# Slot attention: the third tanh moves half a batch later, and VectorE forms the exponents of three of twelve chunks

## The reference

```python
Pn = rmsnorm(P, input_norm_w)              # P: 16 batches x 1500 keys x 128
k_proj = Pn @ Wk.T
v_proj = Pn @ Wv.T
for _ in range(3):
    sn = rmsnorm(slots, slot_norm_w)       # slots: 16 batches x 56 x 128
    q_proj = sn @ Wq.T
    scores = einsum('bkd,bmd->bkm', q_proj, k_proj) * SCALE
    attn = softmax(scores, axis=-2)        # over the 56 slots, for every key
    attn = attn / (sum(attn, axis=-1) + EPS)
    updates = einsum('bkm,bmd->bkd', attn, v_proj)
    slots = gru_cell(updates, slots, ...)  # two sigmoids (as tanh) and a tanh
```

## Time and profile before

| | |
|---|---|
| time, median of 3 runs | 579.34 us (575.66 to 580.33) |
| the profiled execution | 580.25 us, its span 578.4 us |
| slot attention in it | from about 240 us to about 464 us |
| TensorE busy over the span | 443.8 us (77%) |
| VectorE busy | 334.4 us (58%) |
| ScalarE busy | 315.0 us (54%) |
| GpSimd busy | 260.3 us (45%) |

### The profile page before, as it was taken

The page is one execution under the profiler, slowest core; times in us unless marked ns, Lnnn a source line. Parts: engine busy times, 40 slices in busy tenths (PEclk is TensorE's granted clock), DMA queues, the critical chain, the costliest instruction groups (busy, mean ns, idle before and its releaser), DMA issues.

```text
span 578.4 us, 17285 instructions
## 1 busy us (share of the span) xinstructions
PE 443.8 (77%) x6312; PEld 335.0 (58%) x6312; DVE 334.4 (58%) x916; ACT 315.0 (54%) x905; POOL 260.3 (45%) x476
## 2 busy tenths in 40 slices
PE   2893988889679999669999988899998574059910
PEld 1631324556554454458888878888898443049910
DVE  0669964677734655357777766777777326014512
ACT  1573673555412222099999988899999221025400
POOL 9294762223420000236776777766776500700044
PEclk9696996999896999689999999999999855569965
DMA  8862644444149911500000299300000397130112
GB/s 308 304 227 87 218 160 123 135 135 135 54 130 344 342 46 37 255 2 3 3 2 0 82 344 326 118 3 2 0 0 2 124 425 324 55 87 22 40 50 69
DMA packets 47346, 74.10 MB, mean 128 GB/s; under 512 B 4428, under 2 KB 40828, under 8 KB 46140
## 3 DMA queue, kind: packets, MB, share of 16 engines
q1 hardware_dynamic: 42796, 60.51, 31.5%
q0 software_dynamic: 1472, 8.72, 4.2%
q10 hardware_dynamic: 3024, 4.13, 2.3%
HBM read 69.75 MB, written 3.60 MB: 127 GB/s over the span
## 4 chain that ended last, share of the span: by engine, by line
PE 55%; DVE 18%; POOL 9%; issue 7%; ACT 5%; DMA 3%; ACTq 1%; POOLq 1%; DVEq 1%; SPq 0%
PE ps L1582 12%; PE ps L1566 8%; PE ps L1500 5%; PE ps L1408 4%; DVE ps L1207 4%; PE ps L1696 3%; PE ps L1708 3%; PE ps L1516 2%; DVE sm L1218 2%; POOL work L712 2%; POOL xe_scratch L753 2%; PE ps L1380 2%; POOL early_w L758 2%; PE ps L1480 2%; PE ps L1590 1%
## 5 line engine op out<-in xcount | busy, mean ns | idle before, releaser
L867 ACT ACTIVATE work<-ps,nb,rkey 125x56 f32<-125x56 f32 x576 | 173.5, 447 | 5.5 <-DVE nb L1211 5.5
L1566 PE MATMUL ps<-work,region 128*61 128x56 f32 (+1 forms) x2304 | 77.8, 224 | 6.9 <-ACT work L867 5.0
L1566 PEld LDWEIGHTS ps<-work,region 128*61 128x61 f32 (+1 forms) x2304 | 75.6, 140 | 7.5 <-issue 7.4
L1582 PE MATMUL ps<-region,work 125*64 125x129 f32 x1152 | 71.5, 279 | 6.4 <-POOL work L712 3.1
L1582 PEld LDWEIGHTS ps<-region,work 125*64 125x64 f32 x1152 | 65.1, 139 | 11.8 <-POOL work L712 9.3
L712 POOL TENSOR_TENSOR work<-work,rs 125x336 f32<-125x336 f32 x96 | 69.9, 749 | 3.8
L1207 DVE TENSOR_REDUCE ps<-ps 125x12 f32<-125x672 f32 x48 | 41.6, 866 | 36.9 <-PE ps L1566 36.8
L1218 DVE TENSOR_REDUCE sm<-work 125x12 f32<-125x672 f32 x48 | 40.6, 845 | 5.1 <-ACT work L867 4.6
L1408 PE MATMUL ps<-xln,folded 128*128 128x448 f32 x64 | 29.9, 592 | 10.2 <-ACT region L793 10.2
L758 POOL DMA_INDIRECT early_w<-ys_scratch,gidx x14 | 13.3, 950 | 52.1 <-DMA ys_scratch<-folded 48.1
L778 ACT ACTIVATE region<-early_w 125x1536 f32<-125x1536 f32 x16 | 23.7, 1490 | 17.1 <-DVE sumsq L987 12.9
(11 more groups left out here) (290 smaller groups left out, 972.6 us busy)
## 6 DMA issues: line engine op xcount, KB each, us to landing
early_w<-in_ctx SPq DMA_DIRECT2D x16, 768.0 KB, 4.8
region<-in_ctx SPq DMA_DIRECT2D x16, 768.0 KB, 9.4
region<-in_w SPq DMA_DIRECT2D x6, 2048.0 KB, 18.7
region<-in_ctxT SPq DMA_DIRECT2D x16, 750.0 KB, 11.0
work<-in_ctxT_blk SPq DMA_DIRECT2D x22, 187.5 KB
early_w<-in_w POOLq DMA_DIRECT2D x1, 4096.0 KB, 12.3
region<-in_ctx_blk ACTq DMA_DIRECT2D x11, 192.0 KB, 2.8
early_w<-in_ctx_blk ACTq DMA_DIRECT2D x10, 192.0 KB, 2.4
```

The lines of the kernel that those rows point to most:

```text
L867: i = act.activation(shares_of(u, a)[:, h, c, :], ps[:CP, 2 + 2 * a + h, c * S:(c + 1) * S], ACT.Exp, bias=nb[:, a, q:q + 1], scale=rkey[: ...
L1566: mm = pe.matmul(ps[r0:r1, 2 + 2 * a + h, c * S:(c + 1) * S], keysT[:, s, q * CP + r0:q * CP + r1], qT[:, p, a * S:(a + 1) * S], start=Tru ...
L1582: mm = pe.matmul(ps[i * COL:(i + 1) * COL, 6, 0:KW], A[:CP, u, i, h, c * S:c * S + COL], keys[:CP, 2 * p + i, h * CH + c, :], start=(h == ...
```

## The change

Three things are changed, all in slot attention.

1. For the last three chunks of the second half (`BYV = 3`), VectorE works out the exponent, score times `rkey` plus `nb`, right behind `nb` in `maxima`, with one instruction for each chunk, from PSUM into the place of the shares. ScalarE then takes one exponential over these 125 x 168 numbers in place, without scale or bias. A new semaphore `a_lin` tells ScalarE that they are there.
2. `candidate_of`, the third tanh, stands behind the first half of batch 1 on ScalarE, not ahead of it.
3. At the end of a round, `gru_inputs` stands ahead of `slot_mean` on VectorE, and `gru_start` ahead of `slot_proj` on TensorE.

```diff
+BYV = 3
...
+        a_lin = sem("a_lin")
...
                     act.wait_ge(a_neg, n + 1)
                     if later(w, 2):
                         act.wait_ge(u_mm, (w - 1) * 2)
-                for c in range(CH):
+                if h == 1:
+                    act.wait_ge(a_lin, n + 1)
+                for c in range(CH - BYV * h):
                     q = h * CH + c
                     i = act.activation(shares_of(u, a)[:, h, c, :], ps[:CP, 2 + 2 * a + h, c * S:(c + 1) * S], ACT.Exp,
                                        bias=nb[:, a, q:q + 1], scale=rkey[:, b, q:q + 1])
                 if h == 1:
-                    i.then_inc(a_exp, 1)
+                    act.activation(shares_of(u, a)[:, 1, CH - BYV:, :], shares_of(u, a)[:, 1, CH - BYV:, :], ACT.Exp).then_inc(a_exp, 1)
...
                 if now:
                     exponentials(now, v_, 0, 1)
+                    exponentials(now, v_, 1, 0)
                 if old:
                     candidate_of(v_ - 2)
                 if now:
-                    exponentials(now, v_, 1, 0)
                     exponentials(now, v_, 1, 1)
...
                 v.scalar_tensor_tensor(nb[:, a, :], mx, -1.0, rkey[:, b, :], ALU.mult, ALU.mult).then_inc(a_neg, 1)
+                v.wait_ge(a_neg, n + 1)
+                if later(w, 2):
+                    v.wait_ge(u_mm, (w - 1) * 2)
+                for c in range(CH - BYV, CH):
+                    lin = v.tensor_scalar(shares_of(u, a)[:, 1, c, :], ps[:CP, 3 + 2 * a, c * S:(c + 1) * S],
+                                          rkey[:, b, CH + c:CH + c + 1], nb[:, a, CH + c:CH + c + 1], ALU.mult, ALU.add)
+                lin.then_inc(a_lin, 1)
...
                 if following:
                     maxima(following, v_ + 1, 0)
+                if last:
+                    gru_inputs(v_ - 1)
                 if renews(g, c):
                     slot_mean(v_ + 2, c % 2)
-                if last:
-                    gru_inputs(v_ - 1)
...
                 if following:
                     scores(following, v_ + 1, 0)
+                if last:
+                    gru_start(v_ - 1, last[1])
                 if renews(g, c):
                     slot_proj(v_ + 2, (c + 2) % TWO, c % 2)
-                if last:
-                    gru_start(v_ - 1, last[1])
```

## The result

The changed kernel took **591.02 us** (median of 4 runs, 590.24 to 591.74), the kernel before, run beside it, 579.22 us (median of 4). The ratio of the times is **1.0234**, with a 95% interval from 1.0197 to 1.0271. The profiled execution has a span of 589.9 us against 578.4 before: 11.5 us more. The ratios in this text are those on record, with their intervals from single runs; they are not quotients of the medians beside them (here 591.02 / 579.22 = 1.0204) and differ from these by up to 0.4%.

A forecast was written before the change was run, and what follows sets the result against it. The bound was taken to be a chain of waits through TensorE, VectorE and GpSimd, 8.32 us a round, without ScalarE. 22 x 0.50 = 11.0, less 0.6 and 0.7, gave +9.7 us: 589.5 us, range 583.5 to 597.

The forecast's parts named there:

- The price of an instruction: Three new VectorE instructions between `nb` and the sum: 0.155 us each, with the wait 0.50 us a round (0.24 to 0.75).
- 22 rounds: Middle rounds of slot attention: each grows by 0.50 us, 22 x 0.50 = 11.0 us in all.
- second rival: Three instructions cheap, or swallowed in rounds around the change of groups: +3 to +5.8 us, 582 to 585; chance 0.12.
- The beginning: TensorE's 4.68 us wait for the first twelve exponentials: nine and a wide one take 2.99 us, saving 0.6 us.
- The end: Last round, where ScalarE ends last: the sum starts at about 449.7, not 450.43, saving 0.7 us, its own 0.50 included.
- Batch 1's three cost nothing: Middle of VectorE's round: 0.65 us idle ahead of L1207 covers 0.50; at the upper price 0.10 us a round lacks.
- GRU inputs ahead of `ss`, and TensorE's path with `F1w`: End of a round: no gain for the sum; `F1w` products start 0.43 us later, hidden as the chain moves 0.50.
- The third tanh: ScalarE, behind batch 1's `nb`: 0.8 us later, without cost, as new slots and squares have 0.79 us to spare.
- ScalarE: Wide exponential taken at 0.35 us; saves 1.1 us a round off the chain; about 2 us idle a round.
- ScalarE as the bound: ScalarE's 18.03 of 20 us busy sets the round, so relieving it makes the kernel faster, about 571 us; chance 0.05.
- A fallen clock: TensorE idles 0.5 us more a round and its clock falls: over 3 us each round struck, beyond 600; chance 0.04.
- The late slots: Later tanh meets busier GpSimd at group ends, `slot_proj` delays TensorE: 8 rounds by 0.5 to 1 us, 594 to 598; chance 0.06.

The follow-up runs named there:

- batch 0 alone: The changed kernel with exponents on VectorE for batch 0 only, twelve small exponentials on ScalarE for batch 1: 592.82 us, ratio 1.0265.
- batch 1 alone: The changed kernel with exponents on VectorE for batch 1 only, twelve small exponentials on ScalarE for batch 0: 577.11 us, ratio 0.9989.
- behind the sum: The changed kernel with batch 0's three VectorE instructions put after the sum of batch 1, the work the same: 576.35 us, ratio 0.9988.
- the moves alone: The changed kernel with all exponentials on ScalarE as before; third tanh, GRU inputs and GRU start stay moved: 577.55 us, ratio 0.9985.
- constants for both operands: The changed kernel with `rkey` and `nb` replaced by constants in the three VectorE instructions: 584.55 us, ratio 1.0165.
- the split inputs: All exponentials on ScalarE, orders as changed, but second GRU input after sum and `slot_norm`, third gate's product after scores and queries: 575.49 us, ratio 0.997.
- the exponents alone: The changed kernel with its three reorderings undone, keeping the exponents on VectorE and the wide exponential: 591.99 us, ratio 1.0256.

## Why the prediction was right, and where not

- **What bounds the kernel, and by what the change is slower: right.** The exponents lie between `nb` of batch 0 and the sum of batch 1, and that place alone pays (batch 0 alone 1.0265, batch 1 alone 0.9989, behind the sum 0.9988).
- **The price of an instruction: wrong.** The step that failed is "(0.24 + 0.07) / 2 = 0.155 us", a mean between 112 elements and one. The rows of 56 elements say 0.247 us, just above its upper end. It took the number of elements as all that differs, and the three instructions with constants or operands show that operands count as much: 0.123 us for none, and about 0.06 for each. In the kernel's text the GRU input that was taken as one end has one such operand (`wkey`), `ss`, the other end, has none, only a constant: their mean is the price of an instruction with half an operand. As an estimate, one and a half more at 0.06 add 0.09, and 0.155 + 0.09 = 0.245 us stands against 0.247 measured. So the round grew by 0.77 us and not by 0.50, and the sum stands 1.49 us behind `nb` and not some 1.2.
- **The rule that was weighed beside it**, of the Trainium skill (VectorE: DVE Perf Modes, section "The TRN2 errata"), gives 0.18 us as an estimate. The measurement agrees where one operand has a value for each partition (0.187 us), and differs for none (0.123) and for the two of this change (0.247).
- **22 rounds: the other error, which takes back half of the first.** The sum had 22 x 0.50 = 11.0 us; the rows say 14.16. By the true price it would have been 22 x 0.77 = 16.9, that is 5.9 more than forecast, and 2.8 us of that were not charged: 2.3 in the four rounds at the change of groups, 0.5 in the longer round of the loop. The prediction had this in its second rival ("some rounds around the change of groups, where TensorE stops for other reasons") but not in the sum. That the pauses there swallow the delay is read from the distances; no experiment isolates it.
- **The beginning: right**, -0.48 us against -0.6. TensorE's wait of 4.68 us there became two, 0.90 and 3.18, together 0.60 less. Another 0.70 was gone before the part began, where nothing is changed; that is a difference between two executions, not the change's.
- **The end: wrong.** The forecast was -0.7 because the sum would come sooner behind the exponentials. It did not. VectorE's and TensorE's steps of the GRU ended last instead: the wide exponential was done by 462.10, the sum started at 463.62 right behind the second GRU input, and from update 22 to update 23 it took 465.92 - 457.93 = 7.99 us, 7.82 before. The kernel before already had that input just ahead of the sum of 450.43 in the earlier trace rows (first row; the others are the changed kernel's):

```profile
450.04 0.32 DVE L1236 TENSOR_SCALAR work<-ps,bhh 128x112 f32<-128x112 f32 x1
```

```profile
463.37 0.33 DVE L1247 TENSOR_SCALAR work<-ps,bhh 128x112 f32<-128x112 f32 x1
463.62 0.84 DVE L1229 TENSOR_REDUCE sm<-work 125x12 f32<-125x672 f32 x1
```

  At 0.24 us for the input, the sum could have started at 450.28 at the earliest, whatever ScalarE saved: 0.15 us sooner and not 0.7. The 1.44 us that this stretch did gain came from the last update, which took 2.88 us and not 4.49, at another granted clock (below). That is luck, as nothing in the prediction speaks of it.
- **Batch 1's three cost nothing: right, with nothing to spare.** The cover was 0.65 us in the prediction and 0.21 more that it did not count, together 0.86. At the true price it is just used up.
- **GRU inputs ahead of `ss`, and TensorE's path with `F1w`: right.** The sum still follows the same set of instructions, and the moves alone gave 0.9985 (their 0.09 us a round was not foreseen).
- **The third tanh: right.** It started 304.05 - 302.05 = 2.00 us behind `nb` of batch 1, 1.19 before: 0.81 later, as worked out, without cost.
- **ScalarE: right.** The wide exponential took 0.34 in the round above, 0.35 was used; 2 us of idle time a round, as foretold, and absent from the chain. These are ScalarE's exponentials between 260 and 450 us, before and then after (busy us, mean ns | idle ahead of them):

```profile
L867 ACT ACTIVATE work<-ps,nb,rkey 125x56 f32<-125x56 f32 x535 | 161.7, 447 | 5.0 <-DVE nb L1211 5.0
```

```profile
L871 ACT ACTIVATE work<-ps,nb,rkey 125x56 f32<-125x56 f32 x370 | 115.6, 400 | 49.1 <-DVE nb L1215 49.1
L874 ACT ACTIVATE work<-work 125x168 f32<-125x168 f32 x41 | 14.5, 354 | 0.0
```

  What ScalarE saved, 161.7 - 115.6 - 14.5 = 31.6 us, came back as idle time: 49.1 us for `nb` where it was 5.0.

- **The other rivals.** ScalarE as the bound fell with the chain. A fallen clock did not come, though TensorE idled more in every round: every stretch of 20 us from 260 to 460 us in the changed kernel kept 1.00. The late slots did not come either. In one round, the one at 343 to 347 us, `ss` and GpSimd's work behind it do stand in the chain:

```profile
345.57 0.08 DVE ss L1264
...
345.72 0.55 POOL rq L673
346.26 0.55 POOL region L662 x4
346.82 0.17 POOL rs L711
```

  There the sum of batch 1 is not what ends last, GpSimd is, which works on `ss` and copies factors of the keys (L662). But `ss` waits for no `slot_proj`, which is done by 344.2; it stands behind the exponents and the GRU inputs in VectorE's queue. The four rounds around it grew by 0.80 us in all, so this is no further loss that could be told from the exponents'.

## What to carry to other kernels

Ask of an instruction that is to move to an idle engine not how busy that engine is, but what stands behind it in the queue at that place: the same three instructions cost 2.65% between `nb` and the sum and nothing some instructions later. Relieving an engine that isn't in the chain of waits gives it idle time and nothing else. A price for a new instruction is to be taken from a row with the same kinds of operands, not only with the nearest number of elements.

## What the runs showed of the hardware

A VectorE instruction of 56 elements a partition from PSUM cost its queue (start to start) 0.123 us with constants, 0.187 us with one operand that has a value for each partition and 0.247 us with two. On ScalarE an exponential of 168 elements without such operands, not from PSUM, lasted 0.354 us (mean of 41), one of 56 from PSUM with two of them 0.400 in the same kernel; these are durations, and starts of the latter are about 0.3 us apart.

The last update was not the same in all kernels, though its 48 products are. The stretches are, in the kernel before, first the update and then the 4.8 us ahead of it (columns as above, the granted clock third from the end):

```profile
452.70:457.30 4.60, 4.49 (x48) 4.24 (x48) 0.00 (x0) 0.14 (x1) 3.12 (x8) 0.63 0.01 2
447.90:452.70 4.80, 1.78 (x28) 1.38 (x28) 2.98 (x10) 3.35 (x12) 3.46 (x9) 1.00 0.01 3
```

and in the changed one, the update and the 5.1 us ahead of it:

```profile
465.90:468.80 2.90, 2.88 (x48) 2.63 (x48) 0.37 (x2) 0.39 (x1) 2.67 (x6) 1.00 0.01 3
460.80:465.90 5.10, 1.79 (x29) 1.38 (x28) 3.46 (x11) 1.89 (x7) 4.32 (x11) 1.00 0.02 3
```

Before, the granted clock fell to 0.63 on average during the update, which lies between the two levels of 0.5 (1.2 GHz) and 1.00 (2.4 GHz); after, it stayed at 1.00, and 1.61 us were saved. TensorE had been busy for much the same time ahead of it in both, 1.78 of 4.80 us and 1.79 of 5.10. Nor does the wait right ahead of the update tell them apart: with a wait of 1.80 us it took 4.49 us in the kernel before and 4.54 with constants for both operands, but 2.88 with exponents for batch 0 alone. It was long with the moves alone (4.53), with batch 1 alone (4.53) and with the split inputs (5.16) too, and 2.88 with the exponents alone and behind the sum. So up to 2.3 us between two of these profiles can be this one update. With one profile of each kernel, whether it goes with the kernel or with the execution can't be told; what decides is open.
